# The residual part of the node rows, made beside the edge layers or from stored rows beside the first ten sorting steps

## The reference

```python
h = maximum(layernorm(x), 0)
x1 = x + GCN(h)                       # two graph layers over the edges, W1 (64x128), W2 (128x64)
h = maximum(layernorm(x1), 0)
# relation scores of the edges, softmax over the edges of each destination, weighted sum h_nb
out = x1 + leaky(( h + h_nb) @ res_w1.T, 0.01) + leaky((h * h_nb) @ res_w2.T, 0.01)
```

## Time and profile before

| | us |
|---|---|
| median of 3 runs | 4424.13 |
| lowest, highest | 4401.28, 4436.07 |
| span of the profiled execution | 4246.6 |

### The profile page before, as it was taken

The page is one execution under the profiler, slowest core; times in us unless marked ns, Lnnn a source line. Parts: engine busy times, 40 slices in busy tenths (PEclk is TensorE's granted clock), DMA queues, the critical chain, the costliest instruction groups (busy, mean ns, idle before and its releaser), DMA issues.

```text
span 4246.6 us, 40658 instructions
## 1 busy us (share of the span) xinstructions
PE 2075.1 (49%) x10767; PEld 1665.6 (39%) x10767; DVE 2732.3 (64%) x5225; ACT 1412.2 (33%) x2876; POOL 2876.9 (68%) x4049
## 2 busy tenths in 40 slices
PE   6729995565664222122200004543556787676563
PEld 2216663444443121121100003443545666665563
DVE  9947765888886899999933324673776445444442
ACT  0028873332332222222210002211212211887773
POOL 8878867888885888676067776666666400578787
PEclk9969996555555555555555557776776766666665
DMA  6668864444443555555332224324334411122121
GB/s 236 240 234 262 262 233 142 131 133 142 142 140 123 158 171 170 181 171 166 118 78 76 67 69 140 112 59 127 110 96 122 127 56 48 50 67 56 55 57 29
DMA packets 261685, 547.79 MB, mean 129 GB/s; under 512 B 107792, under 2 KB 119930, under 8 KB 261462
## 3 DMA queue, kind: packets, MB, share of 16 engines
q1 hardware_dynamic: 179702, 445.68, 32.1%
q0 software_dynamic: 81760, 99.52, 9.7%
HBM read 275.18 MB, written 273.83 MB: 129 GB/s over the span
## 4 chain that ended last, share of the span: by engine, by line
POOL 50%; issue 19%; DVE 13%; PE 11%; ACT 4%; DMA 3%; POOLq 0%; SPq 0%; DVEq 0%; ACTq 0%
POOL arena L1316 17%; POOL work L1316 14%; POOL result L1311 8%; POOL slot_rows L1311 8%; POOL pause L1324 3%; PE banks L1887 2%; PE banks L1767 2%; PE banks L1896 2%; DMA work<-slot_rows 2%; DVE arena L810 1%; DVE arena L818 1%; PE banks L1868 1%; DVE work L620 1%; DVE arena L614 1%; PE banks L1947 1%
## 5 line engine op out<-in xcount | busy, mean ns | idle before, releaser
L1311 POOL DMA_INDIRECT result<-work,outi x392 | 475.4, 1213 | 368.5 <-DVE work L1018 247.3
L1311 POOL DMA_INDIRECT slot_rows<-work,dsafe x392 | 390.5, 996 | 280.9 <-POOL pause L1329 184.6
L1316 POOL DMA_INDIRECT arena<-g_by_node_and_edge,m_idx x392 | 453.3, 1156 | 168.2 <-POOL pause L1324 105.7
L1316 POOL DMA_INDIRECT work<-in_x,dsafe x392 | 439.6, 1121 | 112.6 <-POOL pause L1324 104.9
L1316 POOL DMA_INDIRECT arena<-h_by_node_and_edge,m_idx x392 | 412.6, 1053 | 111.5 <-POOL pause L1324 59.9
L1759 PE MATMUL banks<-ident,work 128*128 128x128 f32 x392 | 100.5, 407 | 718.9 <-ACT arena L1468 646.2
L1316 POOL DMA_INDIRECT arena<-input_and_place_by_node,src_i x252 | 313.1, 1243 | 74.6 <-POOL pause L1324 73.7
L1759 PEld LDWEIGHTS banks<-ident,work 128*128 128x128 f32 x392 | 68.9, 213 | 742.4 <-issue 662.2
L1854 PE MATMUL banks<-ident,work 128*128 128x128 f32 x556 | 118.0, 353 | 347.2 <-DMA work<-slot_rows 278.5
L1887 PE MATMUL banks<-pos,ident 112*128 112x128 f32 (+3 forms) x784 | 191.7, 385 | 79.1 <-DVE spare L909 58.0
L1958 PE MATMUL banks<-work,ident 128*128 128x65 f32 x784 | 170.8, 413 | 118.9 <-ACT work L1683 118.9
(11 more groups left out here) (332 smaller groups left out, 6861.2 us busy)
## 6 DMA issues: line engine op xcount, KB each, us to landing
slot_rows<-work SPq DMA_DIRECT2D x64, 834.0 KB, 7.9
work<-slot_rows SPq DMA_DIRECT2D x139, 384.0 KB, 3.4
input_and_place_by_node<-arena SPq DMA_DIRECT2D x49, 528.0 KB, 3.0
g_by_node_and_edge<-arena SPq DMA_DIRECT2D x49, 512.0 KB
arena<-x_of_destination SPq DMA_DIRECT2D x56, 448.0 KB, 4.2
work<-g_by_node_and_edge SPq DMA_DIRECT2D x49, 512.0 KB, 4.4
h_by_node_and_edge<-work SPq DMA_DIRECT2D x49, 512.0 KB, 6.6
work<-h_by_node_and_edge SPq DMA_DIRECT2D x56, 448.0 KB, 4.0
```

The costliest lines, as they stand in the source:

```text
L1311: pool.indirect_dma_start(out=table[:, :], out_offset=bass.IndirectOffsetOnAxis(ap=idx, axis=0), in_=of, in_offset=None, bounds_check=boun ...
L1316: pool.indirect_dma_start(out=to, out_offset=None, in_=table[:, :], in_offset=bass.IndirectOffsetOnAxis(ap=idx, axis=0)).then_inc(signal, 16)
```

## The change

Blocks are no longer finished beside the edge layers. step_q keeps q_x1, q_variance, q_h_rows and q_centre, and SP now stores x1 of each block to a new table, x1_by_node, beside h. The steps are 50, of which 26 lie beside E and 24 beside D (so that no step of either holds two). q_result, q_h_turn, q_residual and their two copies are gone from there.

In C, steps 0 to 9 each take some five of the 49 blocks (late_blocks). SP loads h and x1 of a block (three buffers, RX), PE turns h (two banks now) and multiplies by res_w1 (two pairs of banks), ACT copies the turned h and writes 0.01 times the product to SBUF (late_low), DVE takes the maximum of the product in PSUM and that (late_result) and adds x1, SP stores the result. On each engine the late blocks of a step stand at a fixed place in its list: on SP between load_hd(s+1) and load_features(s+2); on DVE between step_c(s+1) and follow(s); on ACT between c_mat(s+2) and follow(s); on PE ahead of the scoring. The late buffers lie in `arena`, where later gathers of C land, so POOL waits after send_rows(10) until the results of all blocks have been stored. Several rings of semaphores for gathered rows are merged into one, `got`, with the counts of the phases added up; this changes no order apart from one wait on gathers that have landed already.

The core of the diff (left out are declarations, the merged semaphores and buffer addresses):

```diff
-QX = 5
-Q_STEPS = NB + 3
-Q_EARLY = 20
+QX = 4
+RX = 3
+Q_STEPS = NB + 1
+Q_EARLY = 26
+LATE_STEPS = 10
...
+        def neighbours_here(eng, s):
+            eng.wait_ge(got[s % 3], SUM2_ALL[s % 3] + 16 * GT * (s // 3 + 1))
         def nodes_done(eng):
             all_landed(eng, q_g1, ROWS_STORED)
             all_landed(eng, q_h, ROWS_STORED)
-            all_landed(eng, q_out, OUT_STORED)
+            all_landed(eng, q_x1s, ROWS_STORED)
+        def late_blocks(s):
+            return range(min(s, LATE_STEPS) * NB // LATE_STEPS, min(s + 1, LATE_STEPS) * NB // LATE_STEPS)
         def step_part(s):
             return max(k for k in range(PARTS) if PART_STEPS[k] <= s)
...
             def leaky(to, of):
                 return stt(out=to, in0=of, scalar=0.01, in1=of, op0=ALU.mult, op1=ALU.max)
-            def q_result(b):
-                dve.wait_ge(Q["os"], 2 * (b + 1))
-                oq.do(leaky(qlk[:, b % 2], qlk[:, b % 2]))
-                after(dve, q_out[b % 2], 16 * (b // 2))
-                tt(qout[:, b % 2], qx[:, b % QX], qlk[:, b % 2], ALU.add).then_inc(Q["out"], 1)
+            def late_result(b):
+                dve.wait_ge(L["low"], 2 * (b + 1))
+                link(tt(rlk[:, b % 2], bank(2 + b % 2 * 2, 2), rlk[:, b % 2], ALU.max), L["leaky"], b + 1)
+                after(dve, r_out[b % 2], 16 * (b // 2))
+                tt(rout[:, b % 2], rx[:, b % RX], rlk[:, b % 2], ALU.add).then_inc(L["out"], 1)
             def step_q(k):
                 if k < NB:
...
-                if k >= 3:
-                    q_result(k - 3)
                 if k < NB:
                     q_centre(k)
...
                     step_c(s + 1)
+                for b in late_blocks(s):
+                    late_result(b)
                 follow(s)
             follow(GE)
...
-                after(sp, Q["out"], b - QX + 1)
+                if b >= QX:
+                    sp.wait_ge(T["centered"], NB + b - QX + 1)
+                    sp.wait_ge(q_x1s[b % 2], 16 * ((b - QX) // 2 + 1))
                 load(qg1_in[:, b % 2], node_block(g1_t, b), q_in[b % 3])
                 for lo, hi in ((0, TAIL_SPLIT), (TAIL_SPLIT, TAIL_P)) if b == NB - 1 else ((0, P),):
                     load(qx[lo:hi, b % QX, :], node_block(x, b, lo, hi), q_in[b % 3])
...
-                if k >= 3:
-                    b = k - 3
-                    sp.wait_ge(Q["out"], b + 1)
-                    for lo, hi in ((0, TAIL_SPLIT), (TAIL_SPLIT, TAIL_P)) if b == NB - 1 else ((0, P),):
-                        load(node_block(out, b, lo, hi), qout[lo:hi, b % 2], q_out[b % 2])
+                if k < NB:
+                    sp.wait_ge(Q["x1"], k + 1)
+                    load(node_block(x1_t, k), qx[:, k % QX], q_x1s[k % 2])
             lanes = slot_t.rearrange("(l s) w -> l (s w)", l=P)
...
+            def load_late(b):
+                after(sp, L["turned"], 2 * (b - RX + 1))
+                after(sp, L["out"], b - RX + 1)
+                load(rh[:, b % RX], node_block(h_t[0:NPAD, :], b), r_in[b % RX])
+                load(rx[:, b % RX], node_block(x1_t, b), r_in[b % RX])
+            def keep_late(b):
+                sp.wait_ge(L["out"], b + 1)
+                for lo, hi in ((0, TAIL_SPLIT), (TAIL_SPLIT, TAIL_P)) if b == NB - 1 else ((0, P),):
+                    load(node_block(out, b, lo, hi), rout[lo:hi, b % 2], r_out[b % 2])
             nodes_done(sp)
             load_features(0)
             load_features(1)
...
                     load_hd(s + 1)
+                if s == 0:
+                    load_late(0)
+                    load_late(1)
+                for b in late_blocks(s):
+                    if b + 2 < NB:
+                        load_late(b + 2)
+                    keep_late(b)
                 if s > 0:
                     load_tiles(s - 1, False)
                 if s + 2 < GE:
...
                 send_rows(s)
+                if s == LATE_STEPS:
+                    pool.wait_ge(L["out"], NB)
+                    all_landed(pool, r_out, OUT_STORED)
                 if s + 3 < GE:
                     get_neighbours(s + 3)
...
-            def q_h_turned(n):
-                act.wait_ge(Q["hturned"], n + 1)
-                after(act, Q["o"], n - 1)
-                copy(qht[:, n % 2], bank(1)).then_inc(Q["ht"], 1)
-            def q_o_rows(n):
+            def late_turned(n):
+                act.wait_ge(L["turned"], n + 1)
+                after(act, L["o"], n - 1)
+                copy(rht[:, n % 2], bank(n % 2)).then_inc(L["ht"], 1)
+            def late_low(n):
                 b, at = n // 2, slice(n % 2 * MM, n % 2 * MM + MM)
-                act.wait_ge(Q["o"], n + 1)
-                after(act, Q["out"], b - 1)
-                copy(qlk[:, b % 2, at], bank(4 + n % 2)).then_inc(Q["os"], 1)
+                act.wait_ge(L["o"], n + 1)
+                after(act, L["out"], b - 1)
+                activation(rlk[:, b % 2, at], bank(2 + b % 2 * 2 + n % 2), ACT.Copy, scale=0.01).then_inc(L["low"], 1)
+            def late_halves(b):
+                if b == 0:
+                    late_turned(0)
+                for n in (2 * b, 2 * b + 1):
+                    if n + 1 < QN:
+                        late_turned(n + 1)
+                    late_low(n)
             def q_root(b):
                 st = q_stat[:, b % 2]
...
-                if 0 <= k - 2 < NB:
-                    for n in (2 * k - 4, 2 * k - 3):
-                        q_h_turned(n)
-                    for n in (2 * k - 4, 2 * k - 3):
-                        q_o_rows(n)
                 if 1 <= k <= NB:
                     q_root(k - 1)
...
                     c_mat(s + 2)
+                for b in late_blocks(s):
+                    late_halves(b)
                 follow(s)
             follow(GE)
...
-            def q_h_turn(n):
+            def late_turn(n):
                 b, half = n // 2, n % 2 * MM
-                pe.wait_ge(Q["hn"], b + 1)
-                after(pe, Q["ht"], n)
+                pe.wait_ge(r_in[b % RX], 32 * (b // RX + 1))
+                after(pe, L["ht"], n - 1)
                 for k in range(4):
-                    ins = transpose(bank(1)[:, k * P:(k + 1) * P], qh[:, b % 2, half + k * P:half + (k + 1) * P], ident[:])
-                ins.then_inc(Q["hturned"], 1)
-            def q_residual(n):
-                pe.wait_ge(Q["ht"], n + 1)
-                after(pe, Q["os"], n - 1)
+                    ins = transpose(bank(n % 2)[:, k * P:(k + 1) * P], rh[:, b % RX, half + k * P:half + (k + 1) * P], ident[:])
+                ins.then_inc(L["turned"], 1)
+            def late_residual(n):
+                b = n // 2
+                pe.wait_ge(L["ht"], n + 1)
+                after(pe, L["leaky"], b - 1)
                 for k in range(4):
                     at = slice(k * P, (k + 1) * P)
-                    ins = matmul(bank(4 + n % 2)[:, at], qht[:, n % 2, at], res1_sb[:], start=True, stop=True)
-                ins.then_inc(Q["o"], 1)
+                    ins = matmul(bank(2 + b % 2 * 2 + n % 2)[:, at], rht[:, n % 2, at], res1_sb[:], start=True, stop=True)
+                ins.then_inc(L["o"], 1)
+            def late_halves(b):
+                if b == 0:
+                    late_turn(0)
+                for n in (2 * b, 2 * b + 1):
+                    if n + 1 < QN:
+                        late_turn(n + 1)
+                    late_residual(n)
             q_turn(0)
             for n in range(QN + 1):
...
             for g in range(GE):
-                for k in beside_e(g):
-                    step_q(k)
                 pe.wait_ge(S["a"], g + 1)
                 e_turn(g, 0)
...
-            for k in range(Q_EARLY, Q_STEPS):
-                step_q(k)
-            pe.wait_ge(Q["os"], QN)
             carried(0, D, 1)
...
             for s in range(GE + 1):
+                for b in late_blocks(s):
+                    late_halves(b)
+                if s == LATE_STEPS:
+                    pe.wait_ge(L["ht"], QN)
+                    pe.wait_ge(L["leaky"], NB)
                 for kind, k, lo, hi in work_at[s]:
                     if kind == "score":
```

56 lines of the change are left out of this document (30 added, 26 removed).

## The result

The changed kernel took 4484.66 us (median of 4 runs, 4463.76 to 4493.39), the kernel before 4430.1 us (4 runs, 4401.28 to 4448.1). The ratio is 1.0129, with a 95% interval from 1.0081 to 1.0177: slower by 1.3%, where 4324 us (4268 to 4388) was forecast. One more run of it on another chip took 4479.87 us beside 4476.82 us for before (median of 7 there), a ratio of 1.001; so the change costs about 1%, or nothing, and gains nothing. Runs of one kernel differ by up to 2%, and the ratios in this document compare its fast runs with the fast ones of before, while the times are medians of all of its runs.

A forecast was written before the change was run, and what follows sets the result against it. POOL was taken to bound E and early C, DVE to bound D. Terms 0 (E), -130 (D) and +30 (early C) took the span from 4246.6 to 4147; with 177.5 around it, 4324 us, eight in ten from 4268 to 4388.

The forecast's parts named there:

- Time around the instructions: Outside the profiled span: 177.5 us, added to the forecast span of 4147 us to give 4324 us.
- E: Edge stage paced by POOL's gathers: six more step_q but 17 results fewer on DVE, counted as 0, with 5 us either way.
- D: Edge stage paced by DVE: the bound passes to POOL, and the stage ends 130 us sooner (bounds 100 and 161).
- the collisions: In D, DVE work lengthening POOL's gathers: 97 us, the middle between 66 at D's own rate and 127 at E's.
- The 1.15 to 1.28 us given as a sign: In D, the mean time of POOL's gathers expected after the change.
- The sums' price in early C: In early sorting, DVE sums of two SBUF inputs lengthen POOL's instructions: 30 us, bounds 10 and 62.
- The late blocks keep pace: In early C, SP's step takes 43 us against POOL's 40.3; the wait after step 10 is free by 28 us.
- The signs of being wrong: In C, POOL idle after step 10 for tens of us or PE's late groups over 7 us a block; or E longer.
- the third: Rival in early C: blocks over 6.5 us delay scoring, nine us per us of loop; 4520 us at 12 a block; chance 0.06.
- its break-even of 57: In early C, the loop length in us that uses up the gain: 9.3 us a block, 4424 us, slower beyond.

The follow-up runs named there:

- the second profile: The kernel before, unchanged, in one more profiled execution: 4459.85 us, span 4458.1 us.
- after: The changed kernel with nothing further altered, in its first profiled execution: 4492.03 us, span 4490.3 us.
- With pauses: The changed kernel with a tiny memset and wait behind every scatter and gather of the sorting stage, three buffers kept: 4368.13 us, ratio 0.987.
- the transfers alone, without pauses: The changed kernel with only the loads and stores of the late blocks, nothing computed, x1 stored as the result: 4277.31 us, ratio 0.966.
- the best kernel: The changed kernel with features asked for mid-way through the late blocks, four buffers, and a pause behind every second transfer of early sorting: 4338.95 us, ratio 0.975.
- first profile of before: The kernel before, unchanged, in the profiled execution the prediction rests on: span 4246.6 us, where its timed runs took 4401 to 4448 us.

## Why the prediction was wrong, point by point

- **Time around the instructions.** 177.5 us were put there, from a median and a span of different executions. It is 1.7 us. In the sum this is a constant and cost nothing. As a reading it hid the cause: the second profile is 211.5 us longer than the first, 161.5 of them in the node stage, where PE waits beside POOL's transfers, and the change was about to put four hand-overs a half block beside such transfers.
- **E: right.** 688.2 and 689.3 us.
- **D: right, a little small.** The end of DVE's work came 2115.29 - 1483.92 = 631 us after the first gather, forecast 1998 - 1347 = 651. The bound did change hands: no gather waits for ACT's copy any more, where it was 54.6 us. The mis-sized term is the collisions: the gathers mean 1109 ns, so (1.109 - 0.95) x 392 = 62 us and not 97. D's own rate gave 66; but the gathers of before mean 1113 ns in its second profile already, so most of that is the execution and not the change. After:

```profile
L1357 POOL DMA_INDIRECT arena<-g_by_node_and_edge,m_idx x392 | 434.8, 1109 | 116.1 <-POOL pause L1365 95.7 <-issue 18.4 <-DMA g_by_node_and_edge<-fix_g,head_m 2.0
...
L631 DVE RECIPROCAL q_stat<-q_stat 128x16 f32<-128x16 f32 x24 | 6.1, 253 | 19.4 <-ACT q_stat L1532 18.9 <-issue 0.6
```

  L631 is the old L607: 19.4/24 = 0.8 us a wait, 0.5 forecast, under 1 as said. The 1.15 to 1.28 us given as a sign were too high.
- **The sums' price in early C: below the 30 us, in the kernel where it can be seen.** In after, POOL waits for ACT, so what its longer instructions cost can't be told. With pauses, where POOL is the bound, the scatters mean 1090 ns with late blocks and 987 without, the gathers 1084 both times: 140 x 0.103 = 14 us. C's steps 0 to 9 are 15 us longer (556, 541). This lies between the forecast's 30 us and the nothing that the Trainium skill's page on SBUF (section Who interferes with whom) infers for tensor_tensor. It is the price of whole late blocks: the transfers alone, without pauses, took the scatters from 1006 to 1040 ns, so the share of the sums is not known, only that it is below the forecast.
- **The late blocks keep pace: wrong; this step decided the sign.** Two of its terms failed. A loop was put at 12 + 7 + 4 x 5.7 + 1 = 43 us; the nine loops of after come to 503 us, 55.9 on the mean, seven of them mostly near 60 and the last two 43. And "nine such steps from 2217" puts step 0 at nothing, though its list has four late blocks ahead of the feature load too: that load came 76 us later. The terms of work are sound where signals are prompt. From the start of the copy L1641 to the end of the first result are 6.7 us (7), in after too; a further block takes 4.9 us on the mean in the best kernel (5.7), and 6.5 with pauses and three buffers, where PE waits for loads to land. In after it takes 9.8. What was missing is the time in which PE's, ACT's and DVE's signals arrive late beside POOL's unbroken transfers: 76 us in step 0 and 7 to 22 us in each of steps 1 to 7. The chain PE, ACT, PE, ACT, DVE has four hand-overs a half block, and can pay at each.
- **The signs of being wrong** came as listed. POOL stood 32.7 us ahead of step 11's scatters, though not at the new wait but for ACT's copy; and late blocks were spaced over 7 us.
- **The rival that came** was the third, the late blocks as the bound, with 0.06. Its number is luck: by its own arithmetic loops of 55.9 us, under its break-even of 57, give 4324 + 9 x (55.9 - 46) = 4413 us, faster than before. The 76 us of step 0, which it lacked as the forecast did, make it 4489, where the ratio gives 4424 x 1.0129 = 4481. What spoke for it was the transfers, and these cost nothing by themselves. The argument against it ("6.0 us of DMA and 5.7 of PE side by side") priced work, and no hand-over.
- **A sign that was there.** Every transfer of E, of D and of the sorting steps from 9 on is followed by a pause; those of early sorting, beside which PE works 1 us in 350, are not. The front part tells both. The question what the pauses are for might have led to the cause. (F's scatters have none either; see the end.)

## What to carry to other kernels

Before work is moved beside another engine's unbroken run of indirect transfers, count its hand-overs between engines, not only its busy time: here a chain of short exchanges lost 5 to 20 us at a time, and 76 us in one step, in a stretch where DMA bandwidth and all engines had room. If it has to be there, try a short rest behind the transfers, each or each second one: it cost some 80 to 90 us by itself here and returned 60 to 115 net. And look at the first step of a loop by itself; its list is often not that of the others. And before a sum is made from a profile, compare its span with the timed runs; where they differ by per cents, the profile is of another kind of execution, and what it lacks may be what the change will meet.

## What the runs showed of the hardware that was not expected

- Signals between PE, ACT and DVE came 2 to 21 us late while POOL issued indirect transfers without a rest, and within 0.1 us or so otherwise. The longest are alike, 21.0 to 21.1 us. A rest is a memset of 0.11 us and the wait for it; it moves the next gather by 0.09 us and the next scatter by 0.59 us.
- Not every unbroken run does it. F issues its 392 scatters without a rest, beside PE busy 361 and ACT 429 of 557 us in the second profile of before, and takes 606 us in the first and 615 in the second. The stretches were seen beside runs with gathers in them.
- Much the same stretches lie in the node stage in spite of a pause behind each gather: 300 to 700 us with PE at 75%, against 95% once POOL had ended.
- The clock of PE goes with it: 0.68 granted in that stretch, and 1.00 after it.
- In the first profile of before the trace has all but 8 of the 10136 semaphore updates of its instructions; in the second, 7747. All later profiles lack 20 to 24% of theirs. So the kind of execution with the hold-ups is also the one whose record of signals has gaps.
- Open: by what way a run of transfers delays the signals, why the first profile of before shows none of it, and how far the recording of a profile takes part. The gaps make the last worth a test; the timed runs have recorded spans too, so they are no control. That the pauses shorten the timed runs as well is measured.
